# Two edge passes and a softmax over all edges, or one pass over groups of four items

## What is computed

```python
h = (x @ W.T).reshape(n, H, D)
h_src = h[src]; h_dst = h[dst]
alpha = einsum('ehd,hd->eh', h_src, a_src) + einsum('ehd,hd->eh', h_dst, a_dst)
enc = relu(edge_attr @ edge_W.T + edge_b).reshape(-1, H, D)
alpha = alpha + sum(enc * h_dst, axis=-1)
alpha = where(alpha >= 0, alpha, 0.2 * alpha)
amax = segment_max(alpha, dst)
ex = exp(alpha - amax[dst])
denom = segment_sum(ex, dst)
attn = ex / maximum(denom[dst], 1e-10)
out = segment_sum(h_src * attn[..., None], dst)
# experts, at the end:
out = out + where(assign == e, probs[:, e] * (H1 @ Wd[e] + bd[e]), 0)
```

## Time and profile before

| what | value |
|---|---|
| median of 3 runs | 4693.37 us (4657.17 to 4708.34) |
| the profiled execution | 4682.37 us, its span 4680.5 us |
| mean granted TensorE clock | 0.896 |
| busy: PE, DVE, ACT, POOL | 78%, 58%, 38%, 39% |
| chain that ended last | PE 27%, issue 21%, POOL 18%, DVE 11%, DMA 11% |

### The profile page before, as it was taken

One profiled execution on the slowest core, in us unless ns is written; L12 is line 12 of the kernel. 1 busy time (PEld: TensorE's weight loads), 2 busy tenths in 40 slices (PEclk: granted clock), 3 DMA queues, 4 the chain that ended last, 5 costly groups with the idle time before them and its releaser, 6 DMA issues.

```text
span 4680.5 us, 74173 instructions
## 1 busy us (share of the span) xinstructions
PE 3645.0 (78%) x17302; PEld 2596.5 (55%) x17303; DVE 2707.9 (58%) x5723; ACT 1787.0 (38%) x4296; POOL 1820.9 (39%) x1972
## 2 busy tenths in 40 slices
PE   4688888667777887788878720788888888908999
PEld 3357777534444444444444410677777777807887
DVE  5657454455655656566556579688888884411111
ACT  2312333233333333333333310666666664422222
POOL 3336666556666766667666600000000000051111
PEclk8889999888889888889888865899999999959999
DMA  4457677667777877778778750688878781131010
GB/s 154 129 188 212 187 220 219 191 189 213 220 225 221 229 218 223 222 223 245 224 222 228 220 131 0 220 263 264 261 262 263 264 263 43 45 104 37 30 33 24
DMA packets 477297, 857.55 MB, mean 183 GB/s; under 512 B 55950, under 2 KB 350288, under 8 KB 475659
## 3 DMA queue, kind: packets, MB, share of 16 engines
q1 hardware_dynamic: 298923, 510.15, 33.2%
q0 software_dynamic: 86352, 241.03, 20.6%
q10 hardware_dynamic: 91778, 103.52, 7.1%
HBM read 589.30 MB, written 266.07 MB: 183 GB/s over the span
## 4 chain that ended last, share of the span: by engine, by line
PE 27%; issue 21%; POOL 18%; DVE 11%; DMA 11%; ACTq 5%; DVEq 5%; ACT 2%; SPq 0%; POOLq 0%
POOL gbuf L523 16%; DMA gbuf<-h_tab,src_t 7%; PE bank L1136 4%; PE bank L1148 4%; PE bank L1096 4%; ACTq L360 4%; DVE wd L1537 3%; PE bank L1031 3%; DVEq L360 2%; PE bank L996 2%; PE bank L1024 2%; PE bank L1013 1%; DVE msg L1526 1%; PE bank L900 1%; DVEq L1531 1%
## 5 line engine op out<-in xcount | busy, mean ns | idle before, releaser
L523 POOL DMA_INDIRECT gbuf<-h_tab,src_t x1568 | 1578.4, 1007 | 953.6 <-issue 402.0
L1074 PE MATMUL bank<-msg,oneh_all 128*125 128x264 f32 x3520 | 814.5, 390 | 97.8 <-DVE msg L1526 97.8
L1394 DVE SCALAR_TENSOR_TENSOR prod<-enc,adst,bank 128x512 f32<-128x512 f32 x880 | 617.9, 743 | 468.0 <-issue 273.2
L761 ACT ACTIVATE enc<-bank,eb 128x512 f32<-128x512 f32 x880 | 555.3, 682 | 756.4 <-PE bank L1024 352.1
L1074 PEld LDWEIGHTS bank<-msg,oneh_all 128*125 128x125 f32 x3520 | 653.0, 188 | 259.2 <-issue 143.1
L1024 PE MATMUL bank<-att,ew_bf 24*128 24x512 bf16 x880 | 287.2, 408 | 376.7 <-ACT enc L761 310.4
L1013 PEld LDWEIGHTS bank<-r,psum 128*128 128x128 f32 x3520 | 520.0, 212 | 80.5 <-issue 18.0
L1526 DVE TENSOR_TENSOR msg<-al,r 128x1056 f32<-128x1056 f32 x440 | 550.5, 1251 | 0.0
L1013 PE MATMUL bank<-r,psum 128*128 128x128 f32 x3520 | 514.3, 294 | 0.4 <-DVE psum L1402 0.4
L817 ACT ACTIVATE dist<-al,dst_f 128x125 f32 x1320 | 425.4, 386 | 83.5 <-ACT oneh_all L821 83.4
L537 POOL TENSOR_TENSOR mvr<-mvr,eps_c 125x2 f32<-125x2 f32 x25 | 4.9, 197 | 1108.4 <-DVE mvr L1577 1108.4
(11 more groups left out here) (252 smaller groups left out, 4723.4 us busy)
## 6 DMA issues: line engine op xcount, KB each, us to landing
al<-spill SPq DMA_DIRECT2D x440, 528.0 KB, 4.6
spill<-gbuf SPq DMA_DIRECT2D x392, 528.0 KB, 5.7
dstb<-dst ACTq DMA_DIRECT2D x440, 125.0 KB
gbuf<-h_tab,src_t POOLq DMA_INDIRECT x1568
att<-attrx ACTq DMA_DIRECT2D x440, 24.0 KB
attrx<-al ACTq DMA_DIRECT2D x8, 1176.0 KB, 12.3
hsplit<-hb POOLq DMA_DIRECT2D x25, 375.0 KB, 6.2
hbt<-hsplit ACTq DMA_DIRECT2D x50, 187.5 KB
```

The costliest lines, as they stand in the source:

```text
L523: pool.indirect_dma_start(gbuf[:, 4 * b + c, :], None, h_tab, bass.IndirectOffsetOnAxis(ap=src_t[:, 4 * s + c:4 * s + c + 1], axis=0)).the ...
L761: m = act.activation(enc[b % 2][:, k, :], bank[k][:, :], ACT.Relu, bias=eb[:, k:k + 1])
L1074: m = pe.matmul(bank[b % NB][0:P, 0:HO], oneh[b % NM][:, c, :], msg[b % NM][:, c, :], start=(c == 0), stop=(c == 3))
L1394: m = v.scalar_tensor_tensor(prod[q][:, k, :], enc[q][:, k, :], adst[:, k:k + 1], bank[2 + 2 * q + k][:, :], ALU.add, ALU.mult)
```

## The change

The two edge passes and the softmax between them become one loop over items, written out in full, with each part of the work delayed by a fixed number of items (lag). Per group of `G` = 4 items:

- POOL gathers an item's rows into one of 16 ring slots (`slot`), where they stay until `m_msg` has read them, 11 items later; there is no spill to HBM and no reload. Gathers are now per item, not per slice: 1760 in place of 1568. They start after stage a's sums are done (7 items) and go on when stage f has ended. `keep_asrc` is in the edge loop only, one per item. Source indices come by a small transfer per item.
- PE sums features of both halves straight from `prod` (no `e_half`), 8 products into quarters of 32 output rows, and adds the source scores by four more (`apad`). All four items of a group gather in bank 7; `e_add` is gone.
- Scores of a group are a 128 x 128 tile. DVE scans it forward and backward for running maxima, carries them over chunk and group ends by short scans on one partition (`g_ends`, `g_chain`, `g_fin`, `g_carry`), with PE turning the ends (`g_up`, `g_down`) and the exponentials (`g_turn`) and ACT copying and taking exponentials (`g_x`, `g_exp`, `g_keep`, `g_fac`). When a group's maximum moves, the open tile's sums are rescaled (`g_scale`).
- Penalties between unlike neighbours and links between chunks are tables in HBM, made before stage b by some 14 DVE instructions; SP loads them with 32 small transfers a group.
- The one-hot of the messages is made wholly by ACT (four instructions and a relu of 500 columns); DVE supplies distances (`m_dt`).
- `m_sum` has one bank, not four, so each item's sum waits for the addition before it (`acc_added`).
- `wd` (the expert weights, 8 MB) is loaded at the end of the edge loop by ACT, not after stage d by SP. The expert bias is added by DVE in `x_keep`, not by PE.

The core of the diff:

```diff
-EB = 10
+EB = 4
-NM = 4
+NM = 3
+RING = 16
+LM = 11
@@ sync
-            for s in range(NS):
-                b = SLOT[s]
-                sp.wait_ge(gathered[b], 64 * USE[s] + 64)
-                sp.dma_start(spill[s].rearrange("p (u c) -> p u c", u=4), gbuf[:, 4 * b:4 * b + 4, 8:HR]).then_inc(spilled[b], 16)
+            def load_links(g):
+                s = item_regs(sp, 0, G * g)
+                wait(sp, x_dif, g - 1)
+                for i in range(G):
+                    for c in range(4):
+                        row = 32 * c + H * i
+                        sp.dma_start(pen[g % 2][row:row + H, 1:128], pen_d[ds(s[i] * SE + 128 * c + 1, 127)].partition_broadcast(H)).then_inc(links_in[g % 2], 16)
+                    for a in range(2):
+                        at0 = 1 - a + 4 * i
+                        for k in range(2):
+                            sp.dma_start(link[g % 2][32 * a:32 * a + 1, k, :, at0:at0 + 4], links[ds(s[i], 1), 2 * a + k]).then_inc(links_in[g % 2], 16)
@@ gpsimd
+            def gather(n):
+                g = n // G
+                if n % G == 0:
+                    pool.wait_ge(idx_in[g % 2], 64 * (g // 2) + 64)
+                wait(pool, gathered[n % NGS], 64 * (n // NGS))
+                wait(pool, msg_ready, n - RING + 1)
@@ tensor
             def e_sum(n):
+                for k in range(KC):
+                    for c in range(4):
+                        pe.matmul(bank[7][32 * c:32 * c + 32, 0:128], hsel[:, i, :], prod[n % 2][:, k, c * 128:(c + 1) * 128], start=(i == 0 and k == 0), stop=False, skip_group_check=True)
+                for c in range(4):
+                    m = pe.matmul(bank[7][32 * c:32 * c + 32, 0:128], apad[:, i, c, :], ident[:, :], start=False, stop=(i == G - 1), skip_group_check=True)
             def m_sum(n):
+                wait(pe, acc_added, n)
@@ vector
+            for k in range(ITEMS + LM + 3):
+                if k % G == 0:
+                    if k + 1 < ITEMS:
+                        t_hot = item_regs(v, 1, k + 1, G)
+                    if 8 <= k < ITEMS + 8:
+                        s_dt, t_dt = item_regs(v, 0, k - 8), item_regs(v, 1, k - 8)
+                    if k >= LM:
+                        n0 = max(0, k - LM - 2)
+                        t_acc = item_regs(v, 1, n0)
...
@@ x stage
-                    pe.matmul(bank[3 + u][:, 0:C], ones_r, bdr[:, ds(e[u] * C, C)], start=False, stop=True).then_inc(y_ready, 1)
+                    v.scalar_tensor_tensor(xo[u][:, 0:C], bdr[:, ds(e[u] * C, C)], xg[u][:, C + 2:C + 3], xg[u][:, 0:C], ALU.mult, ALU.add)
```

More of the change, by code:

```diff
@@ L245, in build_program @@
+        xs, fmax, smax, exr = small[0:4]
+        ex4 = small[4:6]
+        top = sb("top", [1, H], at=mem_e)
+        dl = sb("dl", [1, 2, H], at=mem_e)
+        fac = sb("fac", [P, H], at=mem_e)
         mem_e.close()
         gather_mem.close()
[L249 to L254, removed]
@@ L533, in _ @@
+            clear(edge[32:33, :, 16:17], -BIG)
+            clear(apad[:, :, :, :].rearrange("p i c h -> p (i c h)"), 0.0)
+            pool.wait_ge(tables_stored, 32)
+            for n in range(RING_B, RING_B + 4):
+                gather(n)
+            clear(r1[:, :], 0.0)
+            for n in range(RING_B + 4, ITEMS):
+                gather(n)
             pool.wait_ge(m_used, ITEMS)
@@ new lines, in _ @@
+            for k in range(ITEMS + LM + 2):
+                if k % EB == 0 and k < ITEMS:
+                    t = item_regs(pe, 1, k, EB)
+                if k < ITEMS:
+                    e_enc(k)
+                    e_dst(k, t[k % EB])
+                bank7_read(k)
+                if 0 <= k - 2 < ITEMS:
+                    e_sum(k - 2)
+                elif k % G == 2:
+                    new_sums()
+                if k % G == 3 and 7 <= k <= G * NG + 7:
+                    g_up((k - 7) // G)
+                if (g := group_at(k, 8)) is not None:
+                    g_down(g)
+                if (g := group_at(k, 10)) is not None:
+                    g_turn(g)
+                if 0 <= k - LM - 1 < ITEMS:
+                    m_sum(k - LM - 1)
@@ L1081, in _ @@
+            pe.wait_ge(wr_in, 16 * 7)
             pe.wait_ge(acc_added, ITEMS)
@@ L1534, in m_acc @@
+            def m_acc(n, t):
                 v.wait_ge(m_used, n + 1)
                 wait(v, acc_added, n)
+                if n % G == 0:
+                    v.wait_ge(acc_scaled, n // G + 1)
                 a = acc[:, ds(t, 1), :].rearrange("p t c -> p (t c)")
[L1537 to L1548 removed]
@@ L1667, in x_keep @@
             def x_keep(i):
+                e = nc.values_load_multi_w_load_instructions(
+                    e_row[0:1, ds(2 * i, 2)], engines=[v.engine], min_val=0, max_val=NE - 1,
+                    skip_runtime_bounds_check_because="the row is kept within these bounds")[1]
                 for u in range(2):
@@ L1708 @@
     src_p[:E], dst_p[:E] = np.asarray(src, i32), np.asarray(dst, i32)
+    first, last = dst_p.reshape(NCH, 128)[:, 0], dst_p.reshape(NCH, 128)[:, 127]
+    hsel = np.zeros((128, G, 32), f32)
+    for i in range(G):
+        for h in range(H):
+            hsel[h * 16:(h + 1) * 16, i, H * i + h] = 1
     attr = np.zeros((3, EP), f32)
```

775 lines of the change are left out of this document (384 added, 391 removed).

## The result

The changed kernel takes **4528.7 us** (4518.9 to 4531.6, 4 runs) against 4700.7 (4657.2 to 4708.3): ratio 0.965, 95% interval 0.960 to 0.971. The forecast was 4360, so the sign and the range held, and about half of the gain did not come.

What follows compares the result with a forecast made beforehand. No engine was full in the first edge pass; PE waited for ACT and ran at reduced clock. From 4680.5, -297 to the loop's end, +10 behind it and -37 for experts gave 4356, stated as 4360 us; range 4190 to 4640.

Steps and rivals of the forecast that it cites:

- What a group costs at full clock: Merged edge loop, four items: 24.0 us a group, 6.0 an item, with PE, DVE and POOL each needing about 21.
- PE's wait for DVE: Edge loop, PE's message sum waiting once a group for DVE's addition of the item before: 2.1 us.
- the clock: Edge loop: granted clock over 0.95 despite gaps of 2 us in every group, a third of the earlier gap.
- the last of the three signs: Edge loop: the prediction is wrong if the clock shows half level in each group.
- Rival 2: Edge loop: clock stays at 0.88 as in the first pass, 26.4 us a group, 4617 us in all; chance 0.12.
- SP's price: SP's queue in the edge loop: 36 starts at 0.36 and two loads of 0.3, 13.6 us a group, covered below 0.67.
- Register loads: DVE, per group: aligned four words one fetch, 0.34 us; odd place one a word, 1.4; four loads 3.5.
- rival 3: POOL's gathers shut out by DVE: 5.6 us an item, hidden, or at worst 6.7 and 4660 us; chance 0.10.
- the bias: Expert stage: PE's bias product of 38.9 us goes, DVE's longer step is covered: -37 us.
- Stage f: Ahead of the edge loop: loses ACT's copies and the gathers, a third of PE's 66.6 us wait: -20 us.
- The tables: Before stage b: some 14 DVE instructions for tables, not hidden: +5 us.
- Behind the loop: Stage d: small weights land while the 8 MB of `wd` are under way: +10 us, bounds 0 to 30.

Runs made afterwards that it cites:

- e11: Changed kernel plus eleven unneeded PE products a group in PE's gap, and two link transfers merged into one: 4243.0 us, ratio 0.903 to the kernel before.
- e12: Changed kernel with the two link transfers of one item and direction merged into one, nothing else: 4500.7 us, ratio 0.959 to the kernel before.
- e7: Changed kernel with DVE's register loads only at places divisible by four, spread over three items: 4425.9 us, ratio 0.942 to the kernel before.
- e8: Changed kernel with DVE's register loads aligned and spread, and link transfers merged: 4069.2 us, ratio 0.866 to the kernel before.
- e15: Changed kernel with ACT's 75 small copies of stage f put back, into an unused tile: 4521.6 us, ratio 0.965 to the kernel before.
- e16: Changed kernel with aligned loads, merged links, and DVE's addition ahead of the one-hot and message product: 4151.5 us, ratio 0.884 to the kernel before.
- e2: Changed kernel with DVE's register loads aligned and spread, on a chip where the kernel before takes 4908.8 us: 5570 us, ratio 1.133.

## Why the prediction was right or wrong

**What a group costs at full clock** was forecast at 24.0 and is 23.0 (e11, whose filler fits into the gap). The items were near: quartered sums 0.7 to 0.8 against 1.0, message sums 1.9 to 2.0 against 1.85, DVE's four loads 2.6 against 3.5, its group work 5.6 against 4.4 (scans of 128 columns 0.42 to 0.48, not 0.33; copies and sums on one partition up to 0.39, not 0.2). PE's wait for DVE was put at the right instruction and at 2.1 us of 2.7.

**The step that failed first: the clock.** The working names a gap of 2 us a group, quotes half pace behind a longer gap, and then gives the clock no price, on the ground that the gaps are a third as long. Length was no ground: the gap of 2.7 us drops the clock in 77 of the 78 groups of the window, the last of the three signs that the prediction itself named for being wrong. I had only the one row of 6.55 us and took it for a threshold. Rival 2 was this case with a chance of 0.12. It put a group at 26.4; 25.6 came, since its base was 1.0 too high. So the 1.6 us a group by which the forecast missed are 2.5 for the clock and 0.1 that merged links take away, less 1.0 that the work was cheaper: 1.6 over 107 full groups is 171 of the 205 us. The rest, 34 us, is what this subtraction leaves for groups outside the window and for the loop's two ends, where the forecast had 75 us for the groups without messages or lookups; I did not divide it further.

**The second: SP's price.** 36 starts at the 0.36 of ACT's large transfers made 13.6 us; they take 23.9 or more. The text named the price at which SP would bind, 0.67 a start, and left a factor of two; 24.8 us over 36 starts is 0.69. In the changed kernel that bound stood just behind the clock. It did not cause the miss by itself (e12), but with the gap closed it takes 357 us.

**Register loads.** The forecast price of a load at an odd place, 1.4, measures 0.97, and the aligned one 0.34. Three fetches at 0.32 to 0.34, for words 1, 2 to 3 and 4, would fit the 0.97, and one a word would not. But no rule that I have fits all rows: six words at a place that is 2 over a multiple of four, read above as three fetches, took 1.41 at the middle in the message pass before, and SP's aligned four words take 0.3 or 0.8. That the place matters was right, and it pointed at the stall that mattered: the loads are 2.2 of the 2.7 us of PE's gap, and moving them is the edit that, with merged links, brings 460 us. The Trainium skill (DMA: Bandwidth & Descriptors, Latency and other measured facts) has a floor of about 600 ns; 0.34 lies under it in every one of 321 loads of e7.

**POOL** was rival 3. The changed kernel's gathers take 1.03, as forecast (1.0 to 1.1), hidden. In e8 it is the bound, at 5.4 us an item; rival 3 had a price for it (5.6, hidden) but no case in which all else is faster.

**Outside the loop:** the bias -37, measured -45 and -47. Stage f -20, measured -49: not for the copies themselves (e15); that it was for rows to land is the reading above, without a run. Start of the loop -8, measured -13. The tables +5, measured -4 (the stages up to f end 4 us sooner). Behind the loop +10, measured +22, inside its bounds. Together these 41 us hid a part of the miss, so the total looks better than the loop's forecast was.

## What to carry to other kernels

Price every wait of TensorE twice, once as time and once as clock: here a hole of 2.7 us cost another 2.5 us through the lower level, and useless products in the hole made the kernel 102 us faster. Count the queue that only starts transfers like any engine, at the price of small transfers on that queue. When two unlike edits stop at the same time to the microsecond, the bound lies elsewhere; remove that together with one of them before judging either. On DVE, read table values at places divisible by four and spread the loads.

## What the runs showed of the hardware

- A start on SP takes 0.77 us for `link` (8 pieces of 16 bytes), 0.49 for `idx` (128 pieces of 16 bytes) and 0.44 for `pen` (8 pieces of 508 bytes); one on ACT in the kernel before takes 0.27 to 0.31. What sets the price was not separated.
- After PE's gap of 2.7 us the granted clock is at 1.2 GHz for 3.4 or 10.2 us; in e11, whose gaps are 0.4 a group, never in the window; in e8, with waits of up to 1.8 us, once.
- Four words into DVE's registers: 0.34 at a place divisible by four, 0.97 at an odd one. On SP they took 0.3 or 0.8 at a place divisible by four.
- A gather beside DVE's message product takes 1.2 (e8) to 1.4 us (e16) on average and at most 2.1, in place of 0.95.
- One chip ran the written-out loop (e2) at 3880 us with pauses of PE that have no releaser, while the looped stages behind it took their usual time. Why is open.
